# A second ScalarE pass per weight chunk in the abs-mean reduction of an eight-core transformer layer kernel

## The chip, the cores and the metric

The kernel runs on all eight cores of one Trainium2 chip. Each core works on its own half of one sequence of a batch of four, with no exchange between the cores. The metric is the device time of the slowest core, in microseconds (us). Engines are named as in the profile: PE is TensorE's matmul, PEld its weight load, DVE is VectorE, ACT is ScalarE, POOL is GpSimd and SP is SyncE, which here only issues DMAs.

## The reference

One layer: linear attention, a residual and a layernorm, a feed-forward block with ternary weights, a residual and a layernorm. The input is (4, 4096, 2048) in fp32.

```python
def absmean_quant(w):
    scale = jnp.mean(jnp.abs(w))
    mask = (jnp.abs(w) >= scale * 0.7).astype(w.dtype)
    return jnp.sign(w) * mask
...
sq, sk = elu_plus_one(q), elu_plus_one(k)
kv = jnp.einsum('bhsd,bhse->bhde', sk, v)
qkv = jnp.einsum('bhsd,bhde->bhse', sq, kv)
norm = jnp.einsum('bhsd,bhd->bhs', sq, sk.sum(axis=2))
attn = qkv / (norm[..., None] + EPS)
x = _layernorm(x + attn @ Wo.T)
...
w1_q, w2_q = absmean_quant(w1), absmean_quant(w2)   # 8192x2048 and 2048x8192
h = jax.nn.gelu(x @ w1_q.T + b1, approximate=False)
x = _layernorm(x + h @ w2_q.T + b2)
```

What matters here is `scale`: the mean of |w| over each of two matrices of 16.8 million fp32 values. Nothing can be quantised before it is known.

## The kernel before

Each core runs one long program for its 2048 own tokens. The stages follow one another in the program's text, and each engine takes its instructions in that order; waits are on semaphores. Same-engine results are waited for too: `Prog.op` lets every ScalarE and VectorE instruction wait for the semaphore count that the previous one of its engine left.

**The k/v stage** is a loop of 32 iterations over blocks of 128 tokens (`for sc in range(NSC)`). An iteration has 16 matmuls for k (L300) and 16 for v (L310) into PSUM; on VectorE the bias add (L316), a min (L318) and a max (L320); on ScalarE the exp (L323); on VectorE the sum (L325) and four evictions of v (L332); on TensorE four small matmuls (L344) that add up k-transposed times v. The last line of an iteration is `emit_scale(6)`.

**The q stage** is a loop of 16 iterations over heads (`for ic in range(16)`), each of four groups of 16 matmuls (L435), with L442, L445 and L451 on VectorE and the exp L449 on ScalarE behind each group. `emit_qkv` (L391, L394, L401, L407, L410, L414, L420) follows for the head before. The last line of an iteration is `emit_scale(8)`.

**`emit_scale(n)`** does n jobs of the abs-mean reduction. There are 256 jobs, one for each 128x1024 fp32 chunk (512 KB) of w1 and w2: 192 of them in the k/v stage, 64 in the first eight iterations of the q stage. A job is

- a load of the chunk by SP (L193) into one of two staging slots in `arnE`, chosen by the job's parity, once the job of two before is done with the slot (`sst["abs"][sl]`);
- one ScalarE instruction (L271), which takes the absolute value in place and leaves the sum of each row in `acc_t`, one column for each slot. The profile shows it as an ACTIVATE and an ACTIVATION_READ_ACCUMULATOR. It waits for the load and for the VectorE instruction of the job before;
- one VectorE instruction on a 128x1 column (L278), which subtracts 1024 times 0.7979 from that sum and adds it to `acc1` or `acc2`.

Once all 256 jobs are done, the q stage works out the two thresholds. Behind it come the output projection (L562) with its residual (L577), the first layernorm, and four passes over 512 tokens each through w1 (L751) and w2 (L799). The first of these passes quantises the weights as it goes (L686, L692) and writes them to DRAM; the other three read them back.

Of the kernel before, what the change touches and what calls it, by code (L numbers as in the profile page):

```python
# [9 lines left out]
AF = mybir.ActivationFunctionType  # L10
ALU = mybir.AluOpType
# [12 lines left out]
CBAR = float(np.float32(0.7978845608))  # L24
K1024C = float(np.float32(0.7978845608)) * 1024.0
# [87 lines left out]
def build_nc():  # L113
# [9 lines left out]
    w1 = nc.dram_tensor("w1", [64, 128, 2048], F32, kind="ExternalInput").ap()  # L123
    w2 = nc.dram_tensor("w2", [16, 128, 8192], F32, kind="ExternalInput").ap()
# [53 lines left out]
    p = Prog(nc, es)  # L178
# [6 lines left out]
    sC = p.sem("sC", "scalar")  # L185
# [3 lines left out]
    def dma(qeng, dst, src, waits=()):  # L189
        q = _q[qeng]  # L190
        i = q["rr"]
        q["rr"] = (i + 1) % NLANE
        tok = p.op(qeng, lambda e, a=dst, b=src: e.dma_start(out=a, in_=b),  # L193
                   waits=list(waits) + [q["last"][i]],
                   inc=q["lanes"][i], inc_amt=16)
        q["last"][i] = tok
        return tok

    st_ = {}
    for nm, t_, val in (("ones_m1", ones_m1, 1.0), ("ones_k1", ones_k1, 1.0),  # L200
# [13 lines left out]
                       inc=sV)  # L214
    t_ones_sv = None
    for par in range(2):
        for h in range(KVH):
# [10 lines left out]
                  waits=[t_bkr, st_["ones_k1"]], inc=sT)  # L228
    t_bvmm = p.op("tensor", lambda e: e.matmul(PB[7].ap(), ones_k1.ap(), row(1),
                                               start=True, stop=True),  # L230
                  waits=[t_bvr], inc=sT)
    bkbc, bvbc = Esl(3), Esl(4)
    t_bkbc = p.op("vector", lambda e: e.tensor_copy(bkbc, PB[6].ap()),
                  waits=[t_bkmm], inc=sV)
    t_bvbc = p.op("vector", lambda e: e.tensor_copy(bvbc, PB[7].ap()),
                  waits=[t_bvmm], inc=sV)
# [9 lines left out]
    for dc in range(DC):  # L246
# [8 lines left out]
    sst = {"i": 0, "abs": [None, None],  # L255
           "acc": {"w1": st_["acc1"], "w2": st_["acc2"]}, "done": False}

    def emit_scale(njobs):
        for _ in range(njobs):
            i = sst["i"]  # L260
            if i >= len(scale_jobs):
                break
            sst["i"] += 1
            which, src = scale_jobs[i]
            sl = i % 2
            stage = Esl(5 + 2 * sl, 2)
            acol = acc_t.ap()[:, sl:sl + 1]
            tok_d = dma("sync", stage, src, waits=[sst["abs"][sl]])
            tok_a = p.op("scalar",
                         lambda e, s2=stage, a2=acol:  # L270
                         e.activation(s2, s2, AF.Abs, accum_out=a2),  # L271
                         waits=[tok_d, sst["acc"]["w1"], sst["acc"]["w2"]],
                         inc=sC)
            sst["abs"][sl] = tok_a
            accd = acc1.ap() if which == "w1" else acc2.ap()
            sst["acc"][which] = p.op(
                "vector", lambda e, a2=accd, c2=acol:
                e.scalar_tensor_tensor(a2, c2, K1024C, a2, ALU.subtract, ALU.add),  # L278
                waits=[tok_a], inc=sV)
        if sst["i"] >= len(scale_jobs):  # L280
            sst["done"] = True
# [5 lines left out]
    for sc in range(NSC):  # L287
# [8 lines left out]
        for dc in range(DC):  # L296
# [4 lines left out]
                      waits=[xw[dc], t_wk, kfree[par]],  # L301
                      inc=sT if dc == DC - 1 else None)
# [3 lines left out]
        for dc in range(DC):  # L306
# [4 lines left out]
                      waits=[t_wv, vfree[par]],  # L311
                      inc=sT if dc == DC - 1 else None)
# [14 lines left out]
        for h in range(KVH):  # L327
# [5 lines left out]
                      waits=[tv, t_bvbc], inc=sV)  # L333
# [20 lines left out]
    for h in range(KVH):  # L354
# [3 lines left out]
                       waits=[last_kv_mm], inc=sV)  # L358
# [66 lines left out]
    for ic in range(16):  # L425
        for t in range(NT):
            par = (ic * NT + t) % 2
            tq = None
            for dc in range(DC):
# [6 lines left out]
                          waits=[wq_tok[ic], q_free[par],  # L436
                                 qkv_last_mm[ic - 2] if (t == 0 and ic >= 2)
                                 else None],
                          inc=sT if dc == DC - 1 else None)
# [3 lines left out]
                       waits=[tq, t_bq], inc=sV)  # L443
            m2_ = p.op("vector", lambda e, o=Esl(2), a=PB[par].ap(), b=bqc:
                       e.tensor_scalar(o, a, b, 0.0, ALU.add, ALU.max),  # L445
                       inc=sV)
# [9 lines left out]
        if ic + 2 < 16:  # L456
            wq_tok[ic + 2] = dma("gpsimd", wq_buf(ic + 2), wq[ic + 2],
                                 waits=[tq])
        emit_scale(8)
        if sst["done"] and thr_done is None:  # L460
            slk0 = p.op("vector", lambda e, o=Fst.ap()[:, 0:512]:
                        e.tensor_copy(o, o),
                        waits=[sst["acc"]["w1"], sst["acc"]["w2"], st_["F0"]],
                        inc=sV)
# [3 lines left out]
                       waits=[slk0, t_kv_ev, st_["ones_m1"]], inc=sT)  # L468
# [6 lines left out]
                 waits=[tw1, tw2], inc=sV)  # L475
# [4 lines left out]
                 inc=sV)  # L480
            p.op("vector", lambda e, o=acc_t.ap()[0:1, 0:1],
                 a=tot_sb.ap()[0:1, 0:1]: e.tensor_scalar_mul(o, a, C07),
                 inc=sV)
            p.op("vector", lambda e, o=acc_t.ap()[0:1, 1:2],
                 a=tot_sb.ap()[0:1, 1:2]: e.tensor_scalar_mul(o, a, C07),
                 inc=sV)
# [7 lines left out]
                 inc=sV)  # L494
# [7 lines left out]
                 inc=sV)  # L502
            p.op("vector", lambda e, o=tot_sb.ap()[0:1, 0:1],
                 a=tot_sb.ap()[0:1, 1:2]: e.tensor_scalar_mul(o, a, -1.0),
                 inc=sV)
            p.op("vector", lambda e, o=tot_sb.ap()[0:1, 2:3],
                 a=tot_sb.ap()[0:1, 3:4]: e.tensor_scalar_mul(o, a, -1.0),
                 inc=sV)
            p.op("vector", lambda e, o=Fst.ap()[:, 0:512]: e.tensor_copy(o, o),
                 inc=sV)  # L510
# [5 lines left out]
                        waits=[slk1], inc=sT)  # L516
# [35 lines left out]
    for dc in range(DC):  # L552
        for t in range(NT):
            par = (dc * NT + t) % 2
            two = None
            for icc in range(16):
# [6 lines left out]
                           waits=[wo_tok[dc], attnT_tok[icc], wo_free[par],  # L563
                                  thr_done if (dc == 0 and t == 0) else None],
                           inc=sT if icc == 15 else None)
# [5 lines left out]
                               waits=[xres_free[xs],  # L571
                                      t_bkbc if (dc == 0 and t < 2) else None,
                                      t_bvbc if (dc == 0 and t < 2) else None])
# [4 lines left out]
                      waits=[two, xres_tok[xs], y_free[ys]], inc=sV)  # L578
# [8 lines left out]
                       waits=[ty, sqprev], inc=sC)  # L587
            sqprev = p.op("vector", lambda e, o=Sqsl(t), a=Esl(2):
                          e.tensor_add(o, o, a), waits=[tsq], inc=sV)
        if dc + 2 < 16:  # L590
            wo_tok[dc + 2] = dma("gpsimd", wo_buf(dc + 2), wo[dc + 2],
                                 waits=[wo_mm_done])
# [12 lines left out]
    for t in range(NT):  # L605
        trs = p.op("tensor", lambda e, o=PB[7].ap()[0:1, :], l=ones_m1.ap(),
                   r=Ssl(t): e.matmul(o, l, r, start=True, stop=True),
                   waits=[sqprev, st_free], inc=sT)
        tm = p.op("vector", lambda e, o=row(0), a=PB[7].ap()[0:1, :]:
                  e.tensor_scalar_mul(o, a, 1.0 / 2048.0),  # L610
                  waits=[trs], inc=sV)
        trq = p.op("tensor", lambda e, o=PB[7].ap()[0:1, :], l=ones_m1.ap(),
                   r=Sqsl(t): e.matmul(o, l, r, start=True, stop=True),
                   waits=[tm], inc=sT)
        te2 = p.op("vector", lambda e, o=row(1), a=PB[7].ap()[0:1, :]:
                   e.tensor_scalar_mul(o, a, 1.0 / 2048.0),
                   waits=[trq], inc=sV)
# [330 lines left out]
```

How the kernel before makes its waits and increments, by code:

```python
                def go(eng):  # L95
                    for fn, waits, inc in self.ops[ename]:
                        for h, v in waits:
                            eng.wait_ge(h, v)
                        ins = eng.nop() if fn is None else fn(eng)
                        if inc is not None:
                            ins.then_inc(*inc)
```

## Time and profile before

| | us |
|---|---|
| median of 2 runs | 4753.72 |
| the two runs | 4745.44 and 4762.01 |
| the profiled execution | 4748.2 |
| its span (first to last instruction, slowest core) | 4746.7 |
| spans of the eight cores | 4701.4 to 4746.7 |
| TensorE busy in the span | 3046.7 (64%) |
| VectorE busy | 1588.2 (33%) |
| ScalarE busy | 728.8 (15%) |
| GpSimd busy | 419.8 (9%) |

The times are of whole executions. The busy shares are averages over stages with quite different limits, so they don't say what a longer instruction costs: that is read from the stage in which it stands. All times in the rows further down are us from the start of the span on core 7, the slowest. A timeline row gives the start, the duration, the engine, the line and the operation, then what is written and read, and in square brackets how long the engine had been idle and what ended that.

### The profile page before, as it was taken

To read this page: it belongs to the slowest core of one execution; us is meant where nothing else is said; L and a number is where in the kernel's file an instruction comes from. 1 tells how busy PE (TensorE), PEld (TensorE's weight loads), DVE (VectorE), ACT (ScalarE), POOL (GpSimd) and SP (SyncE) were. 2 spreads that over 40 slices of the span, in tenths; PEclk is the share of its full clock that TensorE was granted. 3 is DMA by queue.
4 is the path that set the end of the run, shared out by engine and by line. 5 is a ranking of instruction groups with operands and counts; after the bars stand their busy time and mean duration, and the time that the engine had idled before them with its cause. 6 is when DMAs were issued, how large, how long until landed. Compare 5 with 4: busy or idle time off the path is not lost.

```text
span 4746.7 us, 40833 instructions; the slowest of 8 cores (4701.4 to 4746.7 us)
## 1 busy us (share of the span) xinstructions
PE 3046.7 (64%) x11722; PEld 1216.6 (26%) x11722; DVE 1588.2 (33%) x2748; ACT 728.8 (15%) x1153; POOL 419.8 (9%) x774
## 2 busy tenths in 40 slices
PE   2455555544776666266664444559995899949996
PEld 0122221111222222022221111123442334413442
DVE  0222222222333333466676566540024001140013
ACT  0344433332221000000000000011100110011100
POOL 1000000000000111022332222100000000000000
PEclk9677777676787888588887777779997999969998
DMA  9756663332011333188885555444443344334442
GB/s 169 181 177 169 181 169 85 84 89 57 14 20 39 103 95 96 56 213 209 222 237 175 168 160 177 134 149 140 155 151 124 124 138 164 133 124 138 156 151 107
DMA packets 215218, 644.51 MB, mean 136 GB/s; under 512 B 30674, under 2 KB 34770, under 8 KB 202708
## 3 DMA queue, kind: packets, MB, share of 16 engines
q1 hardware_dynamic: 161716, 486.66, 34.5%
q0 software_dynamic: 53280, 155.24, 11.8%
q8 instruction: 96, 1.57, 0.1%
q14 instruction: 126, 1.03, 0.1%
HBM read 578.87 MB, written 100.66 MB: 143 GB/s over the span
## 4 chain that ended last, share of the span: by engine, by line
PE 38%; DMA 27%; DVE 19%; ACT 7%; issue 6%; DVEq 1%; POOL 1%; ACTq 0%; SPq 0%; POOLq 0%
PE PB L799 17%; DMA arnE<-w 15%; PE PB L751 12%; PE PB L435 6%; DMA arnE<-xt 6%; DVE arnC L692 5%; DMA arnC<-w1q 3%; DVE arnE L686 3%; ACT arnE L271 3%; PE PB L410 2%; DVE arnE L442 1%; DVEq L98 1%; ACT rows L407 1%; DVE arnE L872 1%; DVE arnB L874 1%
## 5 line engine op out<-in xcount | busy, mean ns | idle before, releaser
L751 PE MATMUL PB<-arnB,arnC 128*128 128x512 bf16 x4096 | 993.2, 400 | 416.6 <-DVE arnC L692 205.4
L799 PE MATMUL PB<-arnA,arnC 128*128 128x512 bf16 x4096 | 943.7, 395 | 304.3 <-DVE arnC L692 304.3
L751 PEld LDWEIGHTS PB<-arnB,arnC 128*128 128x128 bf16 x4096 | 403.0, 102 | 1011.2 <-issue 622.7
L799 PEld LDWEIGHTS PB<-arnA,arnC 128*128 128x128 bf16 x4096 | 411.3, 101 | 836.1 <-issue 392.3
L808 DVE TENSOR_SCALAR arnE<-PB,b_sb 128x512 f32<-128x512 f32 x64 | 48.0, 751 | 1385.5 <-PE PB L799 1385.5
L692 DVE SCALAR_TENSOR_TENSOR arnC<-arnE,thr 128x512 bf16<-128x512 f32 x512 | 384.8, 751 | 93.6 <-DVE arnE L686 32.7
L562 PE MATMUL PB<-arnB,arnC 128*128 128x512 bf16 x1024 | 277.4, 434 | 137.5 <-DVE arnE L577 137.5
L435 PE MATMUL PB<-arnA,arnC 128*128 128x512 bf16 x1024 | 338.4, 505 | 12.7 <-DMA arnC<-wq 10.1
L271 ACT ACTIVATE arnE<-arnE 128x1024 f32<-128x1024 f32 x256 | 270.4, 1056 | 417.7 <-DMA arnE<-w 337.2
L759 ACT ACTIVATE arnA<-PB,b_sb 128x512 bf16<-128x512 f32 x256 | 175.9, 687 | 1001.6 <-PE PB L751 1001.6
L686 DVE TENSOR_SCALAR arnE<-arnE,thr 128x512 f32<-128x512 f32 x512 | 249.6, 488 | 130.9 <-DMA arnE<-w 85.1
L410 PE MATMUL PB<-rows,ones_k 1*128 1x512 f32 x128 | 92.6, 811 | 294.2 <-ACT rows L407 294.2
L278 DVE SCALAR_TENSOR_TENSOR acc<-acc_t,acc 128x1 f32<-128x1 f32 x256 | 40.9, 160 | 574.4 <-ACT arnE L271 570.3
L821 ACT ACTIVATE arnE<-arnB 128x512 f32<-128x512 f32 x64 | 40.3, 630 | 1213.8 <-DVE arnB L812 1213.8
L344 PE MATMUL PB<-arnG 128*128 128x129 bf16 x128 | 18.7, 301 | 295.8 <-DVE arnG L332 295.8
L435 PEld LDWEIGHTS PB<-arnA,arnC 128*128 128x128 bf16 x1024 | 121.4, 124 | 259.4 <-issue 215.1
L562 PEld LDWEIGHTS PB<-arnB,arnC 128*128 128x128 bf16 x1024 | 107.7, 109 | 308.2 <-issue 228.5
L193 POOL DMA_DIRECT2D out<-arnB x64 | 34.6, 540 | 1652.1 <-DVE arnB L874 1652.0
L193 POOL DMA_DIRECT2D w2q<-arnC x256 | 139.1, 543 | 440.3 <-DVE arnE L686 398.6
L193 POOL DMA_DIRECT2D w1q<-arnC x256 | 140.8, 550 | 420.9 <-DVE arnE L686 316.4
L577 DVE TENSOR_TENSOR arnE<-PB,arnE 128x512 f32<-128x512 f32 x64 | 44.3, 692 | 269.5 <-DMA arnE<-xt 255.7
L442 DVE TENSOR_SCALAR arnE<-PB,bq_sb 128x512 f32<-128x512 f32 x64 | 48.1, 751 | 209.9 <-PE PB L435 204.9
(151 smaller groups left out, 1732.6 us busy)
## 6 DMA issues: line engine op xcount, KB each, us to landing
arnE<-w SPq DMA_DIRECT2D x256, 512.0 KB, 4.2
arnE<-w SPq DMA_DIRECT2D x512, 256.0 KB, 4.2
arnC<-w1q SPq DMA_DIRECT2D x192, 512.0 KB, 3.3
arnC<-w2q SPq DMA_DIRECT2D x96, 1024.0 KB, 5.0
w1q<-arnC POOLq DMA_DIRECT2D x256, 128.0 KB, 4.9
w2q<-arnC POOLq DMA_DIRECT2D x256, 128.0 KB, 3.6
arnE<-xt POOLq DMA_DIRECT2D x64, 256.0 KB, 3.9
y1s<-arnE POOLq DMA_DIRECT2D x64, 256.0 KB, 2.4
```

What stands on the lines that cost most here:

```text
L193: tok = p.op(qeng, lambda e, a=dst, b=src: e.dma_start(out=a, in_=b), waits=list(waits) + [q["last"][i]], inc=q["lanes"][i], inc_amt=16)
L271: e.activation(s2, s2, AF.Abs, accum_out=a2),
L410: e.matmul(o, l, r, start=True, stop=True),
L435: e.matmul(o, l, r, start=s, stop=z),
L442: e.tensor_scalar(o, a, b, 0.0, ALU.add, ALU.min),
L562: e.matmul(o, l, r, start=s, stop=z),
L686: e.tensor_single_scalar(o, a, b2, ALU.is_le),
L692: e.scalar_tensor_tensor(o, a, s2, b2, ALU.is_ge, ALU.subtract),
L751: e.matmul(o, l, r, start=s, stop=z),
L759: e.activation(o, a, AF.Gelu, bias=b),
L799: e.matmul(o, l, r, start=s, stop=z),
L808: e.tensor_scalar(o, a, b, None, ALU.add),
```

## The change

The reduction subtracts the expected mean from each element and no longer from each row's sum. For this a job gets a second ScalarE instruction. The first (L271) takes the absolute value in place and sums nothing; the second (L276) adds -0.7979 to each element, in place again, and leaves the row's sum in `acc_t`. The slot is free for the next load, and VectorE may go on, once the second is done. The VectorE instruction (now L283) keeps its form and subtracts 0.0. All lines behind it move down by five.

```diff
             tok_d = dma("sync", stage, src, waits=[sst["abs"][sl]])
+            p.op("scalar",
+                 lambda e, s2=stage:
+                 e.activation(s2, s2, AF.Abs),
+                 waits=[tok_d, sst["acc"]["w1"], sst["acc"]["w2"]],
+                 inc=sC)
             tok_a = p.op("scalar",
                          lambda e, s2=stage, a2=acol:
-                         e.activation(s2, s2, AF.Abs, accum_out=a2),
-                         waits=[tok_d, sst["acc"]["w1"], sst["acc"]["w2"]],
+                         e.activation(s2, s2, AF.Copy, bias=-CBAR,
+                                      accum_out=a2),
                          inc=sC)
             sst["abs"][sl] = tok_a
             accd = acc1.ap() if which == "w1" else acc2.ap()
             sst["acc"][which] = p.op(
                 "vector", lambda e, a2=accd, c2=acol:
-                e.scalar_tensor_tensor(a2, c2, K1024C, a2, ALU.subtract, ALU.add),
+                e.scalar_tensor_tensor(a2, c2, 0.0, a2, ALU.subtract, ALU.add),
                 waits=[tok_a], inc=sV)
```

ScalarE's instructions at the start of the k/v stage, before (x6 means six alike in a row):

```order
L323 ACTIVATE arnE<-arnE 128x512
L271 ACTIVATE arnE,acc_t<-arnE 128x1024 x6
L323 ACTIVATE arnE<-arnE 128x512
L271 ACTIVATE arnE,acc_t<-arnE 128x1024 x6
L323 ACTIVATE arnE<-arnE 128x512
```

And in the changed program, where the exp has become L328:

```order
L328 ACTIVATE arnE<-arnE 128x512
L271 ACTIVATE arnE<-arnE 128x1024
L276 ACTIVATE arnE,acc_t<-arnE 128x1024
L271 ACTIVATE arnE<-arnE 128x1024
L276 ACTIVATE arnE,acc_t<-arnE 128x1024
L271 ACTIVATE arnE<-arnE 128x1024
L276 ACTIVATE arnE,acc_t<-arnE 128x1024
```

Six ScalarE instructions between two exps have become twelve, in pairs. The order of the other engines' instructions and of SP's loads is the same.

## Rows read from the trace of the kernel before

**Rows 1.** The page's costliest groups: line, operation, count, busy, mean ns, idle before.

```profile
L271 ACT ACTIVATE arnE<-arnE 128x1024 f32<-128x1024 f32 x256 | 270.4, 1056 | 417.7 <-DMA arnE<-w 337.2
```

**Rows 2.** Waits of ACT in the k/v stage, 160 to 680 us: total, times, longest.

```profile
ACT arnE L271 <- DMA arnE<-w: 196.9, 116, 3.1
ACT arnE L323 <- DVE arnE L318: 55.0, 30, 2.2
ACT arnE L271 <- DVE acc L278: 47.7, 29, 2.0
```

**Rows 3.** Timeline of ACT: the exps of the third and the last k/v iteration.

```profile
160.18 0.63 ACT L323 ACTIVATE arnE<-arnE 128x512 f32<-128x512 f32 x1 [1.81 <-DVE arnE L318]
...
678.85 0.63 ACT L323 ACTIVATE arnE<-arnE 128x512 f32<-128x512 f32 x1 [1.81 <-DVE arnE L318]
```

**Rows 4.** Timeline of one k/v iteration, ACT and DVE, 303 to 322 us.

```profile
303.05 0.63 ACT L323 ACTIVATE arnE<-arnE 128x512 f32<-128x512 f32 x1 [1.81 <-DVE arnE L318]
303.77 1.06 ACT L271 ACTIVATE arnE<-arnE 128x1024 f32<-128x1024 f32 x1
304.65 1.49 DVE L332 SCALAR_TENSOR_TENSOR arnG<-PB,arnE 128x128 bf16<-128x128 f32 x4
304.74 0.19 ACT L271 ACTIVATION_READ_ACCUMULATOR arnE<-arnE 128x1 f32 x1
306.37 0.16 DVE L278 SCALAR_TENSOR_TENSOR acc<-acc_t,acc 128x1 f32<-128x1 f32 x1 [0.23 <-DVE arnG L332]
306.67 1.06 ACT L271 ACTIVATE arnE<-arnE 128x1024 f32<-128x1024 f32 x1 [1.75 <-DVE acc L278]
308.79 1.06 ACT L271 ACTIVATE arnE<-arnE 128x1024 f32<-128x1024 f32 x1 [0.97 <-DMA arnE<-w]
311.81 1.06 ACT L271 ACTIVATE arnE<-arnE 128x1024 f32<-128x1024 f32 x1 [1.87 <-DMA arnE<-w]
315.10 1.06 ACT L271 ACTIVATE arnE<-arnE 128x1024 f32<-128x1024 f32 x1 [2.15 <-DMA arnE<-w]
318.04 1.06 ACT L271 ACTIVATE arnE<-arnE 128x1024 f32<-128x1024 f32 x1 [1.79 <-DMA arnE<-w]
319.36 0.16 DVE L278 SCALAR_TENSOR_TENSOR acc<-acc_t,acc 128x1 f32<-128x1 f32 x1 [2.78 <-ACT arnE L271]
319.63 0.69 DVE L316 TENSOR_TENSOR arnE<-PB,arnE 128x512 f32<-128x512 f32 x1
321.72 1.06 ACT L271 ACTIVATE arnE<-arnE 128x1024 f32<-128x1024 f32 x1
```

**Rows 5.** SP's load instructions, 160 to 680 us, and their time from issue to landing.

```profile
L193 SPq DMA_DIRECT2D arnE<-w x174: 327/328/328, 162.2 to 677.2; - x174
...
DMA to landing us min/median/max: 3.5/4.2/5.8
```

**Rows 6.** The same for the loads of the first iterations, before 170 us.

```profile
DMA to landing us min/median/max: 4.1/10.9/18.0
```

**Rows 7.** Timeline of one q-stage iteration's end, with its eight jobs, 828 to 855 us.

```profile
828.01 1.06 ACT L271 ACTIVATE arnE<-arnE 128x1024 f32<-128x1024 f32 x1
830.92 0.16 DVE L278 SCALAR_TENSOR_TENSOR acc<-acc_t,acc 128x1 f32<-128x1 f32 x1
831.23 1.06 ACT L271 ACTIVATE arnE<-arnE 128x1024 f32<-128x1024 f32 x1 [2.07 <-DVE acc L278]
848.46 1.06 ACT L271 ACTIVATE arnE<-arnE 128x1024 f32<-128x1024 f32 x1 [1.56 <-DMA arnE<-w]
850.04 0.75 DVE L442 TENSOR_SCALAR arnE<-PB,bq_sb 128x512 f32<-128x512 f32 x1
853.30 2.04 PE L410 MATMUL PB<-rows,ones_k 1*128 1x512 f32 x2 [18.38 <-ACT rows L407]
```

**Rows 8.** Windows of two stages: us, busy of each engine, PE clock, DMA share, GB/s.

```profile
160.18:678.85 518.67, 272.17 (x1028) 113.36 (x1028) 126.79 (x407) 218.19 (x377) 0.00 (x0) 0.74 0.60 177
828.00:886.00 58.00, 30.91 (x80) 10.25 (x80) 15.59 (x28) 17.30 (x28) 0.53 (x1) 0.68 0.29 82
```

**Rows 9.** The page's DMA issues: a load of the same size in a later stage.

```profile
arnC<-w1q SPq DMA_DIRECT2D x192, 512.0 KB, 3.3
```

**Rows 10.** The only table load before the w1 stage, from the instructions of L323.

```profile
L323 ACT ACT_TABLE_LOAD  x1: 1283/1283/1283, 82.6 to 82.6; - x1
```

## The prediction

> **What bounds the kernel now.** I start from the page's costliest groups, to see what the edited instruction costs at present. It runs 256 times for 1056 ns and is busy for 270 us in all, yet ScalarE was idle for 418 us ahead of it, most of that until a load landed [rows 1]. So an idle engine gets more work, and the question is whether that work falls into the idle time or pushes it along. The waits of ScalarE in the k/v stage say what ends the idle time: 116 times the load of a chunk, 29 times the VectorE sum of the job before [rows 2]. The reader should see that TensorE isn't in this list. Its share of the windows row is 272 of 519 us at a granted clock of 0.74 [rows 8], so it has time to spare in this stage.
>
> The timeline of one iteration then gives the chain [rows 4]. I number its six jobs 0 to 5. The exp starts at 303.05, job 0 at 303.77. Job 1 may start only when VectorE has added up job 0, and that small instruction stands behind L332 on VectorE: it runs at 306.37, job 1 at 306.67. From there on the jobs of one slot form a ring. ScalarE finishes job 1, SP issues the next load into the slot, the load lands, job 3 starts at 311.81, and job 5 in the same way at 318.04. After job 5 come L278 (319.36), L316 (319.63), the next exp, and the next job 0 at 321.72. That is one iteration: 2.90 us from job 0 to job 1, two turns of the ring (5.14 and 6.23 us), 3.68 us from job 5 to the next job 0, together 17.95 us. The exps of the third and the last iteration lie 518.67 us apart, which is 29 iterations of 17.89 us [rows 3]: the one shown is typical. So the path of the stage runs through ScalarE, the load and VectorE, and nothing of TensorE is in it.
>
> The q stage with its eight jobs is the same ring with other work around it [rows 7]. Job 0 starts at 828.01, job 1 at 831.23 behind VectorE's L278 of job 0, and jobs 3, 5 and 7 are three turns from there; job 7 starts at 848.46. VectorE can take L442 only behind the last L278, at 850.04, and TensorE has waited 18.38 us when it gets its next row sum to spread, at 853.30. Here too all that lengthens the jobs lengthens the stage.
>
> **The new instruction's length.** Nothing is removed; each job gets one ScalarE instruction more on 128x1024. Its size is that of L271, so 1.056 us [rows 1]. It waits for the one before on the same engine. The exp and job 0 stand in the same relation: 303.05 and 0.63 make 303.68, and job 0 starts at 303.77 [rows 4], a gap of 0.09 us. So a job grows by 1.056 + 0.09 = 1.15 us. The reading of the accumulator (0.19 us) only moves from the first to the second instruction. VectorE's instruction keeps its form and costs nothing more.
>
> The Trainium skill (ScalarE: Activation LUTs, section "What ACT_TABLE_LOAD costs") says that back-to-back ACTIVATEs overlap by about 93 ns. By that rule a job would grow by 0.96 us. The trace has such an overlap only for the accumulator read, which starts at 304.74 while its ACTIVATE lasts to 304.83; between two ACTIVATEs that wait on a semaphore it shows a gap of the same size [rows 4], and I go by the gap.
>
> **What of it lies beside other work.** In an iteration of the k/v stage the second pass of job 0 is covered: it would end at about 304.93 + 1.15 = 306.08, and VectorE is busy with L332 until 306.14 and takes L278 at 306.37 anyway [rows 4]. If that cover went, it would cost 1.15 us an iteration. The second passes of jobs 1, 3 and 5 lie on the chain, one in each of the two turns and one behind the last turn. Those of jobs 0, 2 and 4 lie on the other slot's ring, in time in which ScalarE now waits (0.97 to 2.15 us ahead of each job). Queued behind the waiting second pass are the next job and, after job 5, the next exp; SP's next load and VectorE's L278, with L316 behind it, wait for it.
>
> **What comes back.** The load needs 4.2 us from issue to landing (median of 174; 3.5 at the least) [rows 5], but loads are issued every 17.89/6 = 2.98 us. Two are in flight for over a microsecond of each load. With longer jobs they are issued further apart, by all eight cores, and should land sooner. The bounds are 0 and 4.2 - 3.5 = 0.7 us. I take 0.3: with iterations near 20.7 us the issues lie 3.45 us apart, which still leaves some overlap with a landing time of 3.9, so the least value should not become the rule.
>
> **The sum.**
> - An iteration of the k/v stage: 3 x 1.15 - 2 x 0.3 = 2.85 us. Bounds: 3 x 1.15 = 3.45 with no relief, 3.45 - 1.4 = 2.05 with all of it. Thirty iterations: 85.5 us (62 to 104).
> - The first two iterations run while the token loads fill the queues: the same loads need 10.9 us to land [rows 6]. A later issue may there be made up by a faster landing. Bounds: 0 and 2 x 3.45 = 7 us; I take 3, about the middle.
> - The eight groups of the q stage: three turns and the last pass, 4 x 1.15 - 3 x 0.3 = 3.7 us each, 30 us (4.6 - 2.1 = 2.5 each, 20 us, to 4.6 each, 37 us). Job 0 is covered, for its L278 waits for VectorE until 830.92 anyway [rows 7].
> - TensorE: nothing. In both stages it already restarts from a long wait. The first matmuls after the 18.38 us took 2.04 us [rows 7] at a mean granted clock of 0.68 [rows 8]; some 4 us more of waiting should change nothing. Later stages have the same work in the same order.
>
> Together 85.5 + 3 + 30 = 118.5 us. On the profiled execution's 4748.2 us this is 4866.7. The median of the runs is 5.5 us above that execution, so I expect 4872 us. With all lower bounds the sum is 82 us (4836 us), with all upper ones 148 us (4902 us).
>
> **The rivals.**
>
> *The load queue is the bound, not the ring.* Then loads land every 2.98 us whatever ScalarE does, and the second pass hides in the wait for the next landing; only the last job's pass of each of the 32 + 8 groups remains, 40 x 1.15 = 46 us: 4800 us, which is not slower by 2%. For it speaks that ScalarE waits for a load at nearly every job [rows 2], that two loads overlap, and that the DMA engines are busy at 0.60 and not idle [rows 8]. Against it: 0.60 is not full, and for this the landing time would have to fall by the whole 1.15 us, to 3.05, where the least of 174 is 3.5 [rows 5] and a load of the same size in a quieter stage needs 3.3 [rows 9]. The point from which it decides is a median landing of about 3.1 us. Chance 0.08. A sentence of the Trainium skill (DMA: Bandwidth & Descriptors, section "Latency and other measured facts") points the same way without a size for this case: lighter HBM load makes the fixed cost of a DMA smaller.
>
> *The two passes overlap.* If ScalarE starts the second pass before the first has ended, as it does with the accumulator read, a job grows by about 0.96 us instead of 1.15. That takes 0.19 x (3 x 30 + 4 x 8) = 23 us from the sum: 4849 us, just at the bound of 2%. Against it is the wait for the same engine's count, with its 0.09 us gap [rows 4]. Chance 0.06.
>
> *Copy needs another function table than Abs and Exp.* The one table load of the k/v stage took 1.283 us, for Exp and Abs together [rows 10]. If each job had to switch and switch back, it would grow by 1.15 + 2 x 1.283 = 3.72 us. The chain would have 3 x 3.72 = 11.2 us more in each of 32 iterations and 4 x 3.72 = 14.9 in each of 8 groups, 476 us in all: about 5230 us. For it: the program now takes a third function there that the trace of before doesn't have. Against it: Exp, Abs and Ln run interleaved without a single switch. Chance 0.03. By the Trainium skill (the same page on ScalarE, section "Table sets: the hidden batching unit") cheap functions such as copy and abs are in every set, which would make this nothing.
>
> *The change in the program has another effect on TensorE's clock or on the drift between cores.* Different wait times in the first quarter could leave a different granted clock further on. I have no row that gives it a size beyond the spread of the two runs (16.6 us). Chance 0.01 for a gain of more than 2%.
>
> **How the numbers follow.** A measurement of this kernel can tell about 2% from no change; that is 95 us, 4849 us. The forecast has 0.82, of which 0.07 lies below 4849 (relief near its upper bound). Of the overlap rival's 0.06 half lies on each side. Slower by over 2%: 0.75 + 0.03 + 0.03 = 0.81, rounded up by the part of the clock rival that goes the other way to 0.82. Within 2%: 0.07 + 0.08 + 0.03 less rounding, 0.17. Faster: 0.01. The range is that of the sum's bounds, 4836 to 4902; it leaves out the queue rival and the table loads, together 0.11, and a little at either end.
>
> **What would show it.** ScalarE should have 512 ACTIVATEs of 1056 ns on 128x1024 and 256 accumulator reads, and be busy for 270 us more. In the timeline a second pass should start 1.15 us behind the first. The exps of the third and the last k/v iteration should lie 29 x 20.7 = 601 us apart, and the landing median should be near 3.9 us. In the q stage L442 should come about 25.7 us behind job 0's start, now 22.0. Everything from the output projection on should take as long as before. I am wrong if the landing median stays at 4.2 (then near 4900 us) or goes to 3.1 (4800 us), if table loads stand between the passes, or if the later stages change their length.

## The result and the profile after

The changed kernel is slower. The ratio of its time to that of before is 1.0283, with a 95% interval of 1.0245 to 1.0322. Its profiled execution took 4883.09 us (before: 4748.2), so 134.9 us more; 4872 us was forecast, with a range of 4836 to 4902. The medians of all runs (4958.13 of eleven, and 4755.73 of ten before) contain executions in which one die ran at a lower clock, whatever the kernel; the ratio leaves those out.

| profiled execution | before | after |
|---|---|---|
| us | 4748.2 | 4883.09 |
| span of the slowest core | 4746.7 | 4881.5 |
| spans of the eight cores | 4701.4 to 4746.7 | 4827.0 to 4881.5 |
| ScalarE busy | 728.8 | 999.3 |
| TensorE busy | 3046.7 | 3048.6 |
| VectorE busy | 1588.2 | 1587.7 |

The costliest groups show the new instruction, which answers to [rows 1]. ScalarE has 270 us more work, and L271's idle time ahead has gone from 417.7 to 254.1 us. The idle time ahead of L271 shrank by 164 us and 24 us of new idle time stand ahead of L276, so 140 of the 270 us went into waits that were there anyway, and some 130 pushed the program along (the 24 us are the 0.09 us gap ahead of each second pass, 256 times):

```profile
L271 ACT ACTIVATE arnE<-arnE 128x1024 f32<-128x1024 f32 x256 | 270.5, 1056 | 254.1 <-DMA arnE<-w 194.6
...
L276 ACT ACTIVATE arnE<-arnE 128x1024 f32<-128x1024 f32 x256 | 270.4, 1056 | 23.7 <-ACT arnE L271 0.4
L283 DVE SCALAR_TENSOR_TENSOR acc<-acc_t,acc 128x1 f32<-128x1 f32 x256 | 40.8, 159 | 703.9 <-ACT arnE L276 699.7
```

The exps of the third and the last k/v iteration, from the timeline (as [rows 3]), lie 606.42 us apart on this core, 20.91 us an iteration:

```profile
162.26 0.63 ACT L328 ACTIVATE arnE<-arnE 128x512 f32<-128x512 f32 x1 [1.81 <-DVE arnE L323]
...
768.68 0.63 ACT L328 ACTIVATE arnE<-arnE 128x512 f32<-128x512 f32 x1 [1.81 <-DVE arnE L323]
```

The timeline of one iteration on ScalarE, with the VectorE sums (as [rows 4]); columns are start, duration, what, and the idle time before:

```profile
330.64 1.06 ACT L271 ACTIVATE arnE<-arnE 128x1024 f32<-128x1024 f32 x1
331.79 1.06 ACT L276 ACTIVATE arnE<-arnE 128x1024 f32<-128x1024 f32 x1
...
333.24 0.16 DVE L283 SCALAR_TENSOR_TENSOR acc<-acc_t,acc 128x1 f32<-128x1 f32 x1 [0.23 <-DVE arnG L337]
333.55 1.06 ACT L271 ACTIVATE arnE<-arnE 128x1024 f32<-128x1024 f32 x1 [0.60 <-DVE acc L283]
...
336.92 1.06 ACT L271 ACTIVATE arnE<-arnE 128x1024 f32<-128x1024 f32 x1 [1.08 <-DMA arnE<-w]
...
339.81 1.06 ACT L271 ACTIVATE arnE<-arnE 128x1024 f32<-128x1024 f32 x1 [0.59 <-DMA arnE<-w]
...
343.22 1.06 ACT L271 ACTIVATE arnE<-arnE 128x1024 f32<-128x1024 f32 x1 [1.11 <-DMA arnE<-w]
...
345.69 0.16 DVE L283 SCALAR_TENSOR_TENSOR acc<-acc_t,acc 128x1 f32<-128x1 f32 x1 [3.24 <-ACT arnE L276]
346.00 1.06 ACT L271 ACTIVATE arnE<-arnE 128x1024 f32<-128x1024 f32 x1 [0.48 <-DVE acc L283]
...
350.10 0.63 ACT L328 ACTIVATE arnE<-arnE 128x512 f32<-128x512 f32 x1 [1.81 <-DVE arnE L323]
350.82 1.06 ACT L271 ACTIVATE arnE<-arnE 128x1024 f32<-128x1024 f32 x1
```

The second pass starts 1.15 us behind the first. Job 1 still starts 2.91 us behind job 0, after VectorE's L337: that pass is covered. Jobs 3 and 5 come 6.26 and 6.19 us behind the job before in their slot (5.14 and 6.23 before). But job 5, the last L271 of the six, was not released by its load as before. It was released by VectorE's sum of job 4, which had come late: a chain that the prediction didn't have. It isn't so in every iteration. Of the 232 iterations behind the third exp (29 on each of eight cores), VectorE's sum ended the wait of job 3 in 114 and that of job 5 in 90, where before it did so in 3 and 6; in the others the load did. The waits of ScalarE, 160 to 680 us (as [rows 2]; total, times, longest), show the same shift on this core. The load ends 71 of 125 waits, where before it ended 116 of 145:

```profile
ACT arnE L271 <- DMA arnE<-w: 85.3, 71, 2.5
...
ACT arnE L271 <- DVE acc L283: 26.8, 54, 0.8
```

SP's loads of the k/v stage (as [rows 5]), and the only table load of the stage (as [rows 10]):

```profile
L193 SPq DMA_DIRECT2D arnE<-w x150: 327/328/328, 160.6 to 678.6; - x150
...
DMA to landing us min/median/max: 3.5/3.7/5.0
```

```profile
L328 ACT ACT_TABLE_LOAD  x1: 1283/1283/1283, 81.1 to 81.1; - x1
```

The landings got shorter, from 4.2 to 3.7 us at the median, and no table is loaded between the passes. The end of a q-stage iteration (as [rows 7]) takes 25.45 us from job 0 to L447, against 22.03 before; the forecast was 25.7:

```profile
928.78 1.06 ACT L271 ACTIVATE arnE<-arnE 128x1024 f32<-128x1024 f32 x1
...
932.00 1.06 ACT L271 ACTIVATE arnE<-arnE 128x1024 f32<-128x1024 f32 x1 [0.92 <-DVE acc L283]
...
951.50 1.06 ACT L271 ACTIVATE arnE<-arnE 128x1024 f32<-128x1024 f32 x1 [0.48 <-DVE acc L283]
...
954.23 0.75 DVE L447 TENSOR_SCALAR arnE<-PB,bq_sb 128x512 f32<-128x512 f32 x1
957.49 2.04 PE L415 MATMUL PB<-rows,ones_k 1*128 1x512 f32 x2 [21.80 <-ACT rows L412]
```

The time by stage. The figures are means over the eight cores of times between instructions of the timeline: the exps as above, and VectorE's first evictions of a q-stage iteration. Their sum is the mean of the spans, which grew by 137.6 us; the slowest core's span grew by 134.8.

| us | before | after | more |
|---|---|---|---|
| to the third k/v iteration's exp | 158.6 | 162.2 | 3.6 |
| 29 k/v iterations | 519.2 (17.90 each) | 609.9 (21.03 each) | 90.7 |
| the last iteration, to the first q eviction | 22.6 | 27.1 | 4.5 |
| q stage, 8 iterations with jobs | 445.9 | 475.7 | 29.8 |
| q stage, the 8 iterations without, to their last group's eviction | 309.4 | 309.9 | 0.5 |
| all the rest | 3263.7 | 3272.1 | 8.4 |

The last row isn't the change's doing: in e1 to e11 below, with the same work in that part, it lies between 3242.6 and 3275.7 with no relation to the edit, and the granted clock in it is 0.856 before and 0.854 after. The gain or loss sits where the jobs stand.

### The profile page after: what moved, and what is told of

Its sections match the earlier page's. It is cut to its first block, busy times and chain, and to the rows that moved or that the text cites. A ratio compares the mean times of both kernels' runs of the same rounds, so it can differ in the third digit from the quotient of the medians.

```text
span 4881.5 us, 41345 instructions; the slowest of 8 cores (4827.0 to 4881.5 us)
## 1 busy us (share of the span) xinstructions
PE 3048.6 (62%) x11722; PEld 1217.7 (25%) x11722; DVE 1587.7 (33%) x2748; ACT 999.3 (20%) x1409; POOL 419.9 (9%) x774
## 4 chain that ended last, share of the span: by engine, by line
PE 36%; DMA 26%; DVE 18%; ACT 10%; issue 7%; DVEq 1%; POOL 1%; ACTq 0%; SPq 0%; POOLq 0%
PE PB L804 16%; DMA arnE<-w 14%; PE PB L756 11%; PE PB L440 6%; DMA arnE<-xt 6%; DVE arnC L697 5%; DMA arnC<-w1q 4%; ACT arnE L271 3%; DVE arnE L691 3%; ACT arnE L276 3%; PE PB L415 2%; DMA w1q<-arnC 1%; DVE arnE L447 1%; ACT rows L412 1%; DVEq L98 1%
## 5 line engine op out<-in xcount | busy, mean ns | idle before, releaser
L271 ACT ACTIVATE arnE<-arnE 128x1024 f32<-128x1024 f32 x256 | 270.5, 1056 | 254.1 <-DMA arnE<-w 194.6
L276 ACT ACTIVATE arnE<-arnE 128x1024 f32<-128x1024 f32 x256 | 270.4, 1056 | 23.7 <-ACT arnE L271 0.4
L283 DVE SCALAR_TENSOR_TENSOR acc<-acc_t,acc 128x1 f32<-128x1 f32 x256 | 40.8, 159 | 703.9 <-ACT arnE L276 699.7
L193 POOL DMA_DIRECT2D w2q<-arnC x256 | 140.1, 547 | 445.9 <-DVE arnE L691 395.7
L454 ACT ACTIVATE arnE<-arnE 128x512 f32<-128x512 f32 x64 | 40.3, 629 | 450.1 <-DVE arnE L447 450.1
```

Of the source, the lines that this page charges most:

```text
L271: e.activation(s2, s2, AF.Abs),
L276: e.activation(s2, s2, AF.Copy, bias=-CBAR, accum_out=a2),
```

## The experiments

All figures in this table are from the profiled execution of each kernel; the two stage times are means over the eight cores, as above. The ratio is against the kernel before on the same chip. A dash: no interval came out, or, for e12, the slowest core's span isn't used, since its cores ran at different granted clocks.

| kernel | k/v iteration | 8 q iterations with jobs | slowest core | ratio (95%) |
|---|---|---|---|---|
| before | 17.90 | 445.9 | 4746.7 | |
| after | 21.03 | 475.7 | 4881.5 | 1.0283 (1.0245 to 1.0322) |
| e1, odd jobs two passes | 20.66 | 473.8 | 4862.2 | - |
| e2, even jobs two passes | 19.68 | 456.5 | 4805.1 | 1.0139 (1.0099 to 1.0179) |
| e3, pass off the ring | 18.03 | 441.2 | 4732.9 | 0.9973 (0.9921 to 1.0026) |
| e4, after, 4 slots | 19.08 | 450.0 | 4791.5 | - |
| e5, after, relaxed wait | 20.90 | 463.6 | 4844.9 | 1.0262 (1.0209 to 1.0315) |
| e6, before, 4 slots | 13.70 | 386.4 | 4542.0 | 0.9593 (0.9549 to 0.9637) |
| e7, before, 4 slots, relaxed | 12.70 | 369.1 | 4473.8 | 0.9490 (0.9455 to 0.9525) |
| e8, after, 4 slots, relaxed | 17.25 | 424.6 | 4670.3 | 0.9884 (0.9823 to 0.9945) |
| e9, three passes | 25.79 | 514.7 | 5034.1 | - |
| e10, after, jobs spread | 20.95 | 331.9 | 4695.9 | 0.9963 (0.9902 to 1.0023) |
| e11, before, all three | 12.66 | 309.0 | 4419.9 | 0.9348 (0.9268 to 0.9428) |
| e12, after, all three | 17.25 | 322.3 | - | 0.9677 (0.9563 to 0.9792) |

### e1 and e2: which jobs' passes cost?

The theory was the prediction's: the pass costs where it lengthens the ring of jobs 1, 3 and 5, and nothing on the other slot. Two kernels split the change by the job's parity (e1; e2 has `i % 2 == 0`):

```diff
+            two_pass = i % 2 == 1
+            if two_pass:
...
+            else:
+                tok_a = p.op("scalar",
+                             lambda e, s2=stage, a2=acol:
+                             e.activation(s2, s2, AF.Abs, accum_out=a2),
...
-                e.scalar_tensor_tensor(a2, c2, 0.0, a2, ALU.subtract, ALU.add),
+                e.scalar_tensor_tensor(a2, c2, k2, a2, ALU.subtract, ALU.add),
```

Here `k2` is 0.0 for a job with two passes and 1024 times 0.7979 for one with a single pass.

> Only the jobs with an odd number get the second ScalarE pass; the even ones keep the single pass of before. Ring theory (the prediction's): the second passes of jobs 1, 3 and 5 lie on the chain and those of 0, 2 and 4 in idle time. Then this kernel costs nearly all that the change costs: k/v iterations of 20.7 to 21 us (before 17.9, changed kernel 21.0), some 110 to 130 us in all. Rival (both rings and the hand-over between them share the cost): about half, iterations of 19.3 to 19.6 us and 55 to 80 us in all.

> Only the jobs with an even number get the second pass. Ring theory: hidden, k/v iterations stay within 0.3 us of 17.9 and the time within 0.5% of before. Rival (the hand-over from job 4 to job 5 through VectorE has less slack than a pass is long): iterations of 18.8 to 19.3 us, 35 to 65 us in all.

Odd jobs alone: 20.66 us an iteration, 2.76 of the change's 3.13. Even jobs alone: 19.68 us, 1.78 more than before, and the time 1.39% up. The slowest core's span is 115.5 us longer than before in e1 (110 to 130 expected) and 58.4 us in e2. So the ring theory holds for the odd jobs and falls for the even ones; the rival for e2, a lack of slack in the hand-over from job 4 to job 5, asked for 18.8 to 19.3 and got a little more. The two together would be 4.54 us, but both at once cost 3.13: the costs are not a sum but nearly the later of two chains. The timeline of e2, an iteration on ScalarE, shows the second chain. VectorE's sum releases job 5 in 203 of the 232 iterations (L273 and L278 are an even job's two passes, L284 an odd job's only one, L291 VectorE's sum):

```profile
318.76 1.06 ACT L273 ACTIVATE arnE<-arnE 128x1024 f32<-128x1024 f32 x1 [0.84 <-DMA arnE<-w]
...
321.53 1.06 ACT L284 ACTIVATE arnE<-arnE 128x1024 f32<-128x1024 f32 x1 [0.48 <-DVE acc L291]
...
324.94 1.06 ACT L273 ACTIVATE arnE<-arnE 128x1024 f32<-128x1024 f32 x1 [2.26 <-DMA arnE<-w]
...
331.35 1.06 ACT L273 ACTIVATE arnE<-arnE 128x1024 f32<-128x1024 f32 x1 [2.48 <-DMA arnE<-w]
332.50 1.06 ACT L278 ACTIVATE arnE<-arnE 128x1024 f32<-128x1024 f32 x1
333.82 0.16 DVE L291 SCALAR_TENSOR_TENSOR acc<-acc_t,acc 128x1 f32<-128x1 f32 x1 [4.62 <-ACT arnE L278]
334.12 1.06 ACT L284 ACTIVATE arnE<-arnE 128x1024 f32<-128x1024 f32 x1 [0.48 <-DVE acc L291]
```

Jobs 0, 2 and 4 are the chain here: 6.18 and 6.41 us a turn. Job 5's load is there, and it waits for VectorE to have added up job 4, 2.77 us behind job 4's start. In the kernel before that hand-over had room to spare. Job 4 started at 315.10 and job 5 at 318.04, 2.94 us later [rows 4], where 1.6 us would have done (306.37, the sum of job 0, to 306.67 is 0.30, on top of 1.15 for the job and 0.17 to the sum). The slack was 1.3 us. On the mean of the cores job 4 started 11.26 us behind job 0 before and 13.09 in e2, and it is 1.15 us longer: 2.98 us against a slack of 1.3 leaves 1.7, and 1.78 was measured.

### e3: ScalarE's occupation, or the slot's release?

The kernel before with a pass of the same size after each job, on a tile that nobody uses yet (its values go nowhere). ScalarE does as much as in the changed kernel; only the slot, SP and VectorE don't wait for it.

```diff
             sst["abs"][sl] = tok_a
+            p.op("scalar", lambda e, s2=Fst.ap()[:, 0:1024]:
+                 e.activation(s2, s2, AF.Copy, bias=-CBAR),
+                 waits=[st_["F0"]], inc=sC)
...
```

> The kernel of before, with a pass of the same size and function added after each job's single pass, but on another tile: the slot's next load and VectorE wait for the first pass only. ScalarE is as busy as in the changed kernel. Ring theory: the cost is in the slot's release and not in ScalarE's occupation, so k/v iterations stay at 17.9 to 18.3 us and the time within 1% of before. Rival (ScalarE's occupation is the cost, wherever the pass stands): 21 us an iteration and about 130 us in all.

18.03 us an iteration, and no difference that can be measured in time (0.9973, interval 0.9921 to 1.0026). The page's line of busy times shows the work is there, as much as after (999.3):

```profile
PE 3011.0 (64%) x11489; PEld 1214.4 (26%) x11722; DVE 1587.5 (34%) x2748; ACT 999.1 (21%) x1409; POOL 418.8 (9%) x774
```

In its timeline the idle time ahead of a job has shrunk by about the length of the pass, and the jobs keep their pace:

```profile
317.51 1.06 ACT L271 ACTIVATE arnE<-arnE 128x1024 f32<-128x1024 f32 x1 [0.71 <-DMA arnE<-w]
...
318.76 1.06 ACT L276 ACTIVATE arnF<-arnF 128x1024 f32<-128x1024 f32 x1
...
320.37 1.06 ACT L271 ACTIVATE arnE<-arnE 128x1024 f32<-128x1024 f32 x1 [0.56 <-DMA arnE<-w]
```

So 270 us of ScalarE work are free here, and the same work in front of the slot's release and of VectorE's sum costs 135. That settles the question with which the prediction began. e3 moves the pass behind both at once and doesn't say which of the two costs; e1, e2 and e5 bear on that.

### e4 and e6: more slots

The two further slots lie in the tile for the layernorm statistics, which is unused until the jobs are done. e4 is the changed kernel, e6 the kernel before.

```diff
+    NSL = 4
-    sst = {"i": 0, "abs": [None, None],
+    sst = {"i": 0, "abs": [None, None, st_["F0"], st_["F0"]],
...
-            sl = i % 2
-            stage = Esl(5 + 2 * sl, 2)
-            acol = acc_t.ap()[:, sl:sl + 1]
+            sl = i % NSL
+            stage = Esl(5 + 2 * sl, 2) if sl < 2 else \
+                Fst.ap()[:, (sl - 2) * 1024:(sl - 1) * 1024]
+            acol = acc_t.ap()[:, i % 2:i % 2 + 1]
...
```

> The changed kernel with four staging slots in place of two (the two more lie in the tile for the statistics, unused until then). Ring theory: with the ring gone the next bound is the serial hand-over ScalarE, VectorE, ScalarE of 2.8 us a job: 5 x 2.8 + 4.8 = 18.8 us an iteration instead of 21.0, and some 3.3 us less for each group of eight in the q stage; in all about 90 us less than the changed kernel, 35 to 50 us above before. Rival (the load queue is the bound at about 3.5 us a load in the changed kernel): more slots change nothing, 21 us an iteration.

> The kernel of before with four staging slots. If the two-slot ring sets the 2.98 us between loads before (issue, landing, pass, issue): the hand-over of 1.8 us a job becomes the bound, or the DMA engines at some higher rate, and an iteration falls from 17.9 to 14 to 15.5 us, a group of the q stage by 4 to 6 us, 110 to 150 us in all. If the load queue sets it (the prediction's rival): 17.9 us stay, and landings grow to some 11 us.

e4 came to 19.08 us (18.8 expected), with 25.7 us less in the q stage; the slowest core's span is 90 us shorter than the changed kernel's, as expected. Nearly all its jobs 1 to 5 are now released by VectorE's sum (1134 of 1160). e6 came to 13.70 us, a little below the expected 14 to 15.5, and gained more than expected: the ratio is 0.9593, 205 us on the slowest core. The load queue is not the bound at 2.98 us a load: with four slots a load comes every 2.3 us. Its windows row for 160 to 600 us (us, busy of PE, PEld, DVE, ACT, POOL, PE clock, DMA share, GB/s) has 229 GB/s where before has 177 [rows 8]:

```profile
160.00:600.00 440.00, 279.04 (x1076) 117.35 (x1098) 143.12 (x440) 235.81 (x407) 1.59 (x3) 0.80 0.76 229
```

The landings take longer, not shorter, and four slots hide most of it: 1053 of the 1160 jobs 1 to 5 are still released by VectorE's sum.

```profile
DMA to landing us min/median/max: 3.9/5.3/11.0
```

### e5, e7 and e8: the hand-over through VectorE

A job waits for the VectorE sum of the job before, although each parity has its own column of `acc_t`. The sum of two jobs before is all that it needs:

```diff
-                 waits=[tok_d, sst["acc"]["w1"], sst["acc"]["w2"]],
+                 waits=[tok_d, st_["acc2"], sst["col"][i % 2]],
...
+            sst["col"][i % 2] = sst["acc"][which]
```

> The changed kernel with two slots, but a job waits for the VectorE sum of two jobs before (the one that used its own column of acc_t) and no longer for that of the job before. If the hand-over through VectorE is a part of the chain: job 1 starts 2.3 us behind job 0 instead of 2.8 to 2.9, and a late job 4 no longer holds job 5 for its VectorE sum, so 19.9 to 20.3 us an iteration instead of 21.0 and some 0.9 us less in each group of the q stage, 30 to 40 us in all. If only the slots' rings and the landings count (my step that jobs 0, 2 and 4 don't matter): at most 0.5 us an iteration, under 20 us in all.

> The same with the relaxed wait on VectorE's sum. Job 1 no longer stands behind L332. By the hand-over theory 1 to 1.7 us less an iteration than with four slots alone, unless the DMA engines have become the bound, which would show as equal iterations and a DMA share near 0.9.

> The changed kernel, with both passes, four slots and the relaxed wait. What is left is ScalarE's own time: a job takes 2.3 us, 5 x 2.3 + 4.8 = 16.3 us an iteration (changed kernel 21.0, before 17.9). If that is so, the second pass costs nothing against before: 40 to 70 us less than before in all. If the second pass had a cost of its own beyond ring and hand-over, it stays above before.

e5 is a miss in the k/v stage: 20.90 us an iteration, 0.13 less than after, where the hand-over theory wanted about 1 us less. In the q stage 12.1 us went, where some 7 were expected. Job 7 there starts 0.64 us earlier behind job 0, which is 5 us in eight iterations; the rest isn't explained. The ratio, 1.0262, can't be told from the changed kernel's. Job 1 did start earlier, 2.41 us behind job 0 instead of 2.81 on the mean of the cores, but job 5 stands at 16.02 instead of 16.18: the load for job 3 was issued earlier, lay closer to the one before, and landed 0.3 us later (4.26 instead of 3.95). The hand-over ends the wait in the changed kernel in many iterations, and the odd ring is nearly as long (job 5's load has landed 0.24 us before job 5 starts there); take the one away and the other stays. With four slots the ring is gone and the same edit is worth 1.0 us an iteration (e7 against e6, the low end of the expected 1 to 1.7) and 1.8 us (e8 against e4). In e7 jobs 4 and 5 wait for their loads again and start 0.2 us behind the landing. e8 has both passes and comes to 0.9884 (0.9823 to 0.9945) of the kernel before, some 55 us less (40 to 70 expected). Against the same form without the second pass it is slower, by 4.2% (0.9884 over e7's 0.9490): once the other waits are gone the pass costs 4.5 us an iteration, more than the 3.13 of the change itself.

What e8 still pays is ScalarE's own time. It was to take 16.3 us an iteration and took 17.25. The first of the 29, at 143 us, still shares the queues with the token loads and takes about 29 us; the mean of the others is 16.83. In them jobs start 2.39 us apart and not 2.3, since the next job waits for the accumulator read; 5 x 0.09 us is most of the difference.

### e9: three passes

```diff
+            p.op("scalar",
+                 lambda e, s2=stage:
+                 e.activation(s2, s2, AF.Abs),
+                 inc=sC)
             tok_a = p.op("scalar",
```

> The changed kernel with one more ScalarE pass per job (the absolute value a second time): three passes, two slots. If a pass cost 1.15 us on each of three places and nothing new came up, an iteration would be 21.0 + 3.45 = 24.5 us. By the hand-over theory a job is now 3.95 us from start to start of the next (three passes, VectorE's sum), and six of them in a row need 5 x 3.95 + 6.0 = 25.8 us, more than the two rings: 25.5 to 26 us an iteration, nearly no wait for loads left.

25.79 us an iteration, where 25.8 was worked out from the hand-over and 24.5 by adding 1.15 three times. In the timeline each job starts 3.93 us behind the one before, released by VectorE's sum. That is so for 1094 of the 1160 jobs 1 to 5; the load releases the others:

```profile
303.35 1.06 ACT L271 ACTIVATE arnE<-arnE 128x1024 f32<-128x1024 f32 x1 [0.48 <-DVE acc L287]
304.50 1.06 ACT L276 ACTIVATE arnE<-arnE 128x1024 f32<-128x1024 f32 x1
305.65 1.06 ACT L280 ACTIVATE arnE<-arnE 128x1024 f32<-128x1024 f32 x1
307.28 1.06 ACT L271 ACTIVATE arnE<-arnE 128x1024 f32<-128x1024 f32 x1 [0.48 <-DVE acc L287]
```

The third pass costs 4.76 us an iteration where the second cost 3.13. The load's wait, which had swallowed a part of the second, was used up.

### e10, e11 and e12: the block of eight jobs in the q stage

```diff
                 emit_qkv(ic - 1, t)
+            emit_scale(2)
...
-        emit_scale(8)
```

> The changed kernel with the eight jobs of a q-stage iteration spread out, two behind each of the four groups of matmuls. A group without jobs takes 9.7 us, two jobs 5.6 us of ScalarE and VectorE, and the loads have time to land. If the q stage pays for the jobs because they stand in one block, its first eight iterations fall from 476 to 330 to 380 us, the k/v stage stays at 21.0 us, and the time falls by 100 to 140 us, to about that of before. If ScalarE's work itself counts there, it stays above 440 us.

> The kernel of before with four slots, relaxed wait and spread jobs. The first eight q iterations fall from 369 to 320 to 340 us; 30 to 50 us less than with slots and wait alone.

> The changed kernel with four slots, relaxed wait and spread jobs. First eight q iterations from 425 to 330 to 350 us, 75 to 95 us less than with slots and wait alone, about 4580 us. The second pass then still costs ScalarE's own time in the k/v stage, some 4.5 us an iteration against the best form of before.

With the jobs spread, the changed kernel's first eight q iterations take 331.9 us instead of 475.7, at the lower end of what was expected, and the kernel is back at the time of before (0.9963, 0.9902 to 1.0023). Its slowest core's span is 186 us shorter than the changed kernel's, more than the 100 to 140 expected. The spread edit gives 144 of it; the stages that it doesn't touch are 29 us shorter on the mean of the cores, within the spread of that row above. In its timeline a group of matmuls with two jobs takes 9.78 us (863.99 to 873.77), and TensorE waits 2.92 us for the row that ScalarE makes, as before in a group without jobs (the one at 1199.77 us waits 2.92 us, too):

```profile
863.99 5.31 PE L440 MATMUL PB<-arnA,arnC 128*128 128x512 bf16 x16
...
866.13 1.06 ACT L271 ACTIVATE arnE<-arnE 128x1024 f32<-128x1024 f32 x1 [0.92 <-DVE acc L283]
867.28 1.06 ACT L276 ACTIVATE arnE<-arnE 128x1024 f32<-128x1024 f32 x1
...
872.74 1.09 PE L415 MATMUL PB<-rows,ones_k 1*128 1x512 f32 x2 [2.92 <-ACT rows L412]
873.77 5.31 PE L440 MATMUL PB<-arnA,arnC 128*128 128x512 bf16 x16
```

So 144 us of what the q stage paid for its jobs came from their standing in one block. What the second pass still costs the q stage in the best form is small, but e12 doesn't give it well. In its profiled execution four cores (0, 1, 6, 7) had a granted clock of 0.79 to 0.81 in that stage and took 313.8 to 317.1 us; the other four had 0.70 to 0.74 and took 325.1 to 332.6. Against e11's 309.0 at 0.79 it is about 6 us at a like clock (an estimate from those four cores), 13 on the mean of all cores, where it had been 30. The rows of 664 to 986 us on cores 0 and 2 (as [rows 8]):

```profile
664.00:986.00 322.00, 211.64 (x628) 73.49 (x626) 126.74 (x237) 200.97 (x282) 4.23 (x8) 0.80 0.41 111
...
664.00:986.00 322.00, 226.34 (x601) 75.68 (x610) 120.03 (x220) 200.49 (x280) 4.23 (x8) 0.70 0.42 113
```

In the k/v stage the same cores ran at 0.68 to 0.78 and took 17.20 to 17.28 us an iteration, with no relation to the clock: TensorE isn't on the chain there.

With all three edits the kernel before comes to 0.9348 of its time (e11; its spread gave 60 us in the q stage, to 309.0 where 320 to 340 were expected, and the slowest core's span is 54 us shorter than e7's, with 30 to 50 expected) and the changed one to 0.9677 (e12; 322.3 us in the q stage on the mean, below the 330 to 350 expected). So in the best form the second pass costs some 3.5% (0.9677 over 0.9348), more than the 2.8% that it cost in the old one. The second pass still costs 4.6 us an iteration in the k/v stage there, as expected.

## Why the prediction was right, and where it was not

**The chain.** Right in what it said of the length of a pass (1.15 us, as it started), of ScalarE's occupation (e3: free), of job 0's pass (covered in both stages) and of TensorE (out of it, as the clocks of e12 show for the k/v stage). The sum was 118.5 us; 134.9 came.

**The term that was mis-sized is the k/v iteration.** It was given as 3 x 1.15 - 2 x 0.3 = 2.85 us and measured 3.13 over 29 iterations. Two things are in the difference. First, the relief. The landing median fell by 0.5 us, more than the 0.3 that I took, but what counts are the loads on the chain, those for jobs 3 and 5. As means over the cores they landed in 4.09 and 4.29 us before and in 3.95 and 3.92 after: 0.51 together, where I had 0.6. The loads for jobs 0, 1 and 4 gained more (0.57, 0.45 and 0.54 us), and those for jobs 0 and 1 land in time for nothing, since their jobs start over a microsecond behind the landing anyway. Second, the step that the second passes of jobs 0, 2 and 4 lie in idle time. It is false: e2 shows 1.78 us for them alone. In the changed kernel it cost less, because the odd ring had grown as much; jobs 3 and 5 start 0.17 us later behind their landings than before (0.13 and 0.04). Together 0.09 + 0.17 = 0.26 of the missing 0.28 us. That it came out near was luck in part: two chains grew by like amounts, and I had priced one.

**The first iterations** were given 3 us and took 3.6. **The q stage** was given 30 us and took 29.8. The odd jobs' passes alone cost it 27.8 us (e1) and the even ones' 10.6 (e2), so there too a second chain stood close behind the one that I priced. **The rest**: 4.5 us for the last iteration where 2.85 was counted, and 8.4 and 0.5 us in stages that the change doesn't touch, for which the sum had nothing. On the mean of the cores that is 137.6 us. Without those 8.9 us it would be 128.7, nearer to the 118.5 than the whole shows.

**The rivals.** The load queue as the bound (0.08) is refuted by e6: the same queue gives a load each 2.3 us once there are slots. The overlap of the passes (0.06) is refuted by the timeline: 331.79 is 1.15 us behind 330.64, for a duration of 1.056. By the rule of the Trainium skill (ScalarE: Activation LUTs, "What ACT_TABLE_LOAD costs") it would have been 0.96; between two ACTIVATEs of which the second waits for the first's count the trace disagrees. The table switches (0.03) didn't come: the trace has one table load, at 81.1 us. With that the Trainium skill agrees, by the same page's section "Table sets: the hidden batching unit". A clock that shifts the later stages didn't show: 0.856 before and 0.854 after.

## What to carry to other kernels

An instruction on an idle engine is free or costs up to its whole length by what waits for it, not by how busy the engine is: place it behind the release of the buffer and not in front of it, and count the turns of the ring between two fixed points. Where two rings alternate on one engine, give both a length and take the later; the slack of the one that is early is the first thing to be used up, and removing one of two equal chains gains next to nothing (0.13 us an iteration in e5). Before paying for a longer job, look for a third buffer and for a wait that asks for more than it needs: with four slots and a wait on the right column the kernel with the extra pass is 1.2% faster than the old one without. That doesn't make the pass free. With those waits gone it costs more than it did at first, 3.5 to 4.2% instead of 2.8%.

## What the runs showed of the hardware that I had not expected

- A load's time to land depends on how many are in flight, well below a full DMA (share 0.48 to 0.76): 512 KB take 3.7 us at the median at 151 GB/s (two slots, one load each 3.5 us), 4.2 at 177 GB/s and 5.3 at 229 GB/s (four slots, one each 2.3 us). The least was 3.5 to 3.9 us in all of them. The rate still grew, by 29%, when the landing grew by a quarter. The rate alone doesn't make it: in e4, with four slots and one load each 3.2 us, it was 169 GB/s, less than before, and the median was 5.0 us.
- In e3 ScalarE did 270 us more and the time didn't move by what can be measured, in neither direction. VectorE was busy for 1587.5 us (1588.2 before) and the landing median was 4.3 us (4.2 before), so the ACTIVATEs on another tile slowed neither.
- The granted clock was lower where the waits had grown: it was 0.745 before and 0.708 after in the k/v stage, and 0.687 and 0.674 in the q stage's first half (means over the cores); behind them it was the same within 0.002. In the k/v stage a lower clock costs nothing, as e12's cores show; what it costs the q stage no run separates. TensorE's first matmuls after 21.80 us of waiting took 2.04 us, the same as after 18.38.
